# Gates made by VectorE's 32x32 block transposes, and the T1 sums moved from GpSimd to VectorE

## The reference, cut to what matters

```python
def _L1_ffn_ref(x, base_W, router_W, lora_A, lora_B):
    base = jnp.einsum('bsd,od->bso', x, base_W)
    logits = jnp.einsum('bsd,ed->bse', x, router_W)
    probs = jax.nn.softmax(logits.astype(jnp.float32), axis=-1)
    top_vals, top_idx = jax.lax.top_k(probs, 2)
    rw = top_vals / jnp.sum(top_vals, axis=-1, keepdims=True)
    w_dense = jnp.sum(jax.nn.one_hot(top_idx, 8) * rw[..., None], axis=-2)
    mid = jnp.einsum('bsd,edr->bser', x, lora_A)      # 8 experts x rank 16
    mid = mid * w_dense[..., None]
    return base + jnp.einsum('bser,erd->bsd', mid, lora_B) * 2
x = x + _L0_ffn_ref(_L0_cond_ref(x, ...), ...)
x = x + _L1_ffn_ref(_L1_cond_ref(x, ...), ...)
```

## Time and profile before

| | us |
|---|---|
| median of 3 runs | 687.29 |
| lowest and highest | 687.27, 687.53 |
| the profiled execution, first to last instruction | 685.8 |
| TensorE matmuls busy in it | 680.0 (3309 matmuls) |
| VectorE busy | 421.5 |
| ScalarE busy | 233.5 |
| GpSimd busy | 261.3 |
| granted TensorE clock | 1.000 throughout |

### The profile page before, as it was taken

The page is one execution under the profiler, slowest core; times in us unless marked ns, Lnnn a source line. Parts: engine busy times, 40 slices in busy tenths (PEclk is TensorE's granted clock), DMA queues, the critical chain, the costliest instruction groups (busy, mean ns, idle before and its releaser), DMA issues.

```text
span 685.8 us, 9221 instructions
## 1 busy us (share of the span) xinstructions
PE 680.0 (99%) x3309; PEld 600.7 (88%) x3309; DVE 421.5 (61%) x705; ACT 233.5 (34%) x429; POOL 261.3 (38%) x217
## 2 busy tenths in 40 slices
PE   8999999999999999999999999999999999999997
PEld 7999999888888888888899999998888888888886
DVE  5664668768855473862663753886698437738423
ACT  6444245644131034220514344266252302422200
POOL 2373023027593150395133432030647625105920
PEclk9999999999999999999999999999999999999999
DMA  8355756992868934547742755689836886535633
GB/s 298 109 159 180 261 198 209 390 380 108 263 186 321 343 117 130 157 141 258 281 170 72 231 169 183 246 275 375 332 122 216 291 333 195 175 117 171 192 113 122
DMA packets 74131, 147.24 MB, mean 215 GB/s; under 512 B 6948, under 2 KB 38308, under 8 KB 73958
## 3 DMA queue, kind: packets, MB, share of 16 engines
q1 hardware_dynamic: 70678, 138.20, 59.0%
q10 hardware_dynamic: 1872, 6.36, 3.0%
q0 software_dynamic: 1536, 2.10, 1.1%
HBM read 98.42 MB, written 47.33 MB: 213 GB/s over the span
## 4 chain that ended last, share of the span: by engine, by line
PE 97%; DMA 1%; SPq 1%; ACT 0%; DVE 0%; issue 0%
PE ps L599 45%; PE ps L481 15%; PE ps L482 15%; PE ps L483 15%; PE ps L558 4%; PE ps L615 2%; DMA e_raw<-in_ext 1%; PE ps L608 1%; SPq L281 0%; PE ps L498 0%; PE ps L581 0%; ACT e_hl L710 0%; SPq L258 0%; DVE w_hl L972 0%; DVE w L1177 0%; ACT w_hl L719 0%
## 5 line engine op out<-in xcount | busy, mean ns | idle before, releaser
L599 PE MATMUL ps<-x_hl,a_hl 128*128 128x512 f32 x1344 | 317.7, 394 | 0.0
L599 PEld LDWEIGHTS ps<-x_hl,a_hl 128*128 128x128 f32 x1344 | 251.1, 188 | 53.6 <-issue 0.3
L481 PE MATMUL ps<-e_hl,w_hl 128*128 128x384 f32 (+1 forms) x432 | 145.8, 338 | 0.6 <-DVE e_hl L972 0.5
L482 PE MATMUL ps<-e_hl,w_hl 128*128 128x384 f32 (+1 forms) x432 | 145.8, 338 | 0.0
L483 PE MATMUL ps<-e_hl,w_hl 128*128 128x384 f32 (+1 forms) x432 | 145.6, 337 | 0.0
L481 PEld LDWEIGHTS ps<-e_hl,w_hl 128*128 128x128 f32 x432 | 81.5, 189 | 1.8 <-issue 1.0
L482 PEld LDWEIGHTS ps<-e_hl,w_hl 128*128 128x128 f32 x432 | 81.4, 188 | 0.0
L483 PEld LDWEIGHTS ps<-e_hl,w_hl 128*128 128x128 f32 x432 | 81.4, 188 | 0.0
L972 DVE TENSOR_TENSOR x_hl<-x_raw,x_hl 128x512 fp32r<-128x512 f32 x64 | 60.8, 1004 | 8.9 <-ACT x_hl L806 8.9
L1353 POOL TENSOR_TENSOR w<-x_raw 128x512 f32<-128x512 f32 x16 | 23.8, 1515 | 104.6 <-DMA x_raw<-in_xT 34.0
L972 DVE TENSOR_TENSOR w_hl<-w_raw,w_hl 128x1024 fp32r<-128x1024 f32 (+2 forms) x24 | 20.6, 869 | 57.2 <-ACT w_hl L697 50.3
(11 more groups left out here) (115 smaller groups left out, 900.1 us busy)
## 6 DMA issues: line engine op xcount, KB each, us to landing
a_hl<-form_scratch SPq DMA_DIRECT2D x112, 512.0 KB, 5.2
form_scratch<-f_hl SPq DMA_DIRECT2D x56, 512.0 KB, 7.4
e_raw<-in_ext SPq DMA_DIRECT2D x12, 580.0 KB, 8.6
w_raw<-in_w ACTq DMA_DIRECT2D x12, 512.0 KB, 3.3
x_raw<-in_xT SPq DMA_DIRECT2D x6, 1024.0 KB, 8.0
x_raw<-x_scratch SPq DMA_DIRECT2D x6, 1024.0 KB, 7.0
x_scratch<-x_raw SPq DMA_DIRECT2D x16, 256.0 KB, 3.1
out_T<-x_raw SPq DMA_DIRECT2D x16, 256.0 KB, 3.3
```

The costliest lines, as they stand in the source:

```text
L481: nc.tensor.matmul(dst, w_hi, m_hi, start=start, stop=False, skip_group_check=again)
L482: nc.tensor.matmul(dst, w_hi, m_lo, start=False, stop=False, skip_group_check=again)
L599: last = nc.tensor.matmul(ps[:, bank, :], a_hl[:, n % NM, k, w, :], x_hl[:, slot, k, x, :], start=start and i == 0, stop=i == 3 * KH - 1, ...
```

## The change

The router's eight columns are copied 16 times side by side into a stationary tile `rt_cols` (ScalarE, one copy for each chunk). One 128x512 matmul ahead of the inner matmul then gives each token's logits 16 times over the partitions. VectorE's block transpose turns this into `by_token` [128, 16 groups, 32]: 32 tokens of a group on a quarter of the partitions, the eight logits beside each other. `routing` works on [128, 16, 8] instead of [128, 4, 8], finds the maxima by reduce and compare instead of max and index, writes the gates into `by_token` and transposes them by blocks again into `hg`. `gated` then reads the inner product from PSUM directly. Logit products, gate transposes, ScalarE's copy `inner` and GpSimd's `make_t1` are gone; VectorE makes T1.

```diff
             def inner_low(l, g, tb):
...
+                pe.wait_ge(S["rt_done"], u + 1)
+                nc.tensor.matmul(ps[:, S_BANK, :], rt_cols[:], low_mv[tb][:], start=True,
+                                 stop=True).then_inc(S["pe_logit"], 1)
                 nc.tensor.matmul(ps[:, H_BANK, :], stack[tb][:, D:D + ER], low_mv[tb][:], start=False,
                                  stop=True).then_inc(S["pe_h"], 1)
...
             def product(g, j, m, bank, start):
...
-                if gates_of is not None:
-
-                    pe.wait_ge(S["h_done"], 2 * g + gates_of + 1)
-                    pe.wait_ge(S["gate_done"], 2 * g + gates_of + 1)
...
-                    if logits_of is not None and i < TT:
-                        tb = logits_of
-                        logit = nc.tensor.matmul(ps[:, S_BANK, i * NE:(i + 1) * NE], low_mv[tb][:, i * P:(i + 1) * P],
-                                                 stack[tb][:, D + ER:EXT], start=True, stop=True)
...
-                    if gates_of is not None and i < TT:
-                        gate = nc.tensor.transpose(ps[:, H_BANK, i * P:(i + 1) * P], gates[:, i, :], ident_sb[:])
...
                         for m in (m2, m2 + 1):
                             pe.wait_ge(S["w5_done"], KH * g + m + 1)
                             product(g, W3, m, BANK_C12[m], False)
-                            if m == 0:
-                                pe.wait_ge(S["hg_lo"], 2 * g + 2)
-                            low_and_experts(0, 1, m, BANK_C12[m])
+                            if m >= 2:
+                                low_and_experts(0, 1, m, BANK_C12[m])
+                        if m2 == 0:
+                            pe.wait_ge(S["hg_lo"], 2 * g + 2)
+                            for m in range(2):
+                                low_and_experts(0, 1, m, BANK_C12[m])
...
+            def router_cols(l, g, tb):
...
+                if u:
+
+                    act.wait_ge(S["hg_done"], u)
+                nc.scalar.copy(rt_cols[:].rearrange("p (n e) -> p n e", e=NE),
+                               stack[tb][:, D + ER:EXT].bitcast(f32).unsqueeze(1).broadcast_to([P, P // NE, NE])
+                               ).then_inc(S["rt_done"], 1)
...
                     adapters(l, g, 1, more)
-                    t1_split(g, range(2))
-                    inner(g, 1)
-                    t1_split(g, range(2, 3))
+                    router_cols(l, g, 1)
+                    t1_split(g)
                     top_exp(g, 1)
-                    t1_split(g, range(3, 4))
                     keep_w5(g, 0)
...
+            def make_t1(g):
+
+                dve.wait_ge(S["pe_hx"], 2 * g + 2)
+                for k in range(KH):
+                    dve.wait_ge(S["t2_done"], KH * g + k + 1)
+                    sub(x_sum[:, SLOT_OF[g % SUPER][T1], k, 1, :], raw_of(B22, k), c21[:, k, :]
+                        ).then_inc(S["t1_done"], 1)
...
+                ins = nc.vector.transpose(by_token[:].rearrange("p g c -> p (g c)"), ps[:, S_BANK, :])
+                ins.then_inc(S["logit_read"], 1)
+                dve.wait_ge(S["logit_read"], u + 1)
+                chain(nc.vector.tensor_tensor(lg, lg,
+                                              bias_r[:].unsqueeze(1).broadcast_to([P, GR, NE]), ALU.add))
+                for i, (v, m, gate) in enumerate(((lg, ma, ga), (lg2, mb, gb))):
+                    chain(nc.vector.tensor_reduce(top[i][:], v, AXIS.X, ALU.max))
+                    chain(nc.vector.tensor_tensor(m[:], v, over(top[i], NE), ALU.is_equal))
+                    if i:
+                        sub(gap[:], top[1][:], top[0][:]).then_inc(S["gap_done"], 1)
+                    chain(nc.vector.tensor_tensor(m[:], m[:], ranks, ALU.mult))
+                    chain(nc.vector.tensor_reduce(first_of[i][:], m[:], AXIS.X, ALU.max))
+                    if i == 0:
+                        chain(nc.vector.tensor_tensor(m[:], over(first_of[i], NE), ranks, ALU.is_equal))
+                        chain(nc.vector.scalar_tensor_tensor(lg2, m[:], -3.0e38, lg, op0=ALU.mult, op1=ALU.add), False)
+                    chain(nc.vector.tensor_tensor(gate[:], over(first_of[i], WANT), wanted, ALU.is_equal))
                 dve.wait_ge(S["exp_done"], u + 1)
                 chain(nc.vector.tensor_scalar(den[:], ex[:], 1.0, None, ALU.add))
                 chain(nc.vector.reciprocal(wb[:], den[:]))
                 chain(nc.vector.tensor_scalar(wa[:], wb[:], 2.0, None, ALU.mult))
...
+                chain(nc.vector.tensor_tensor(den[:], ex[:], wa[:], ALU.mult), False)
+                chain(nc.vector.tensor_tensor(ga[:], ga[:], over(wa, WANT), ALU.mult))
+                chain(nc.vector.tensor_tensor(gb[:], gb[:], over(den, WANT), ALU.mult))
+                chain(nc.vector.tensor_tensor(by_token[:].rearrange("p g (n r) -> p g n r", r=R),
+                                              *(m[:].unsqueeze(3).broadcast_to([P, GR, WANT, R]) for m in (ga, gb)),
+                                              ALU.add))
+                chain(nc.vector.transpose(hg[:], by_token[:].rearrange("p g c -> p (g c)")))
...
+                dve.wait_ge(S["pe_h"], u + 1)
+                nc.vector.scalar_tensor_tensor(hg[:], ps[:, H_BANK, :], bias_sb[:, KT:KT + 1], hg[:],
                                                op0=ALU.add, op1=ALU.mult).then_inc(S["hg_done"], 1)
-                dve.wait_ge(S["hg_hi"], u + 1)
+
+            def gated_low(g, tb):
+                dve.wait_ge(S["hg_hi"], 2 * g + tb + 1)
                 sub(hg_hl[:, tb, 1, :], hg[:], hg_hl[:, tb, 0, :].bitcast(f32)).then_inc(S["hg_lo"], 1)
...
                     low_rest(g, 1)
+                    make_t1(g)
                     out_c11(g, 2)
                     out_c11(g, 3)
-                    made_split(g, T1, range(2))
-                    routing(g, 1)
-                    made_split(g, T1, range(2, 4))
-                    sum_split(g, T3, w57)
-                    for m in range(KH):
+                    made_split(g, T1)
+                    sum_split(g, T3, w57)
+                    routing(g, 1)
+                    gated(g, 1)
+                    keep_u2(g, 0)
+                    gated_low(g, 1)
+                    for m in range(1, KH):
                         keep_u2(g, m)
-                    gated(g, 1)
```

More of the change, by code:

```diff
@@ L39 @@
 SUPER = NCH // 2
+SQ = 32
+GR = CH // SQ
+WANT = SQ // R
 CHAIN = 13
@@ L185, in fused_layers @@
         assert 2 * E_PITCH <= 5 * CH
-        gates = place("gates", [P, TT, ER], f32, at[0] - CH * 4)
-        h_sb = place("h_sb", [P, CH], f32)
+        by_token = place("by_token", [P, GR, SQ], f32)
+        rt_cols = place("rt_cols", [P, P], f32r, at[0] - CH * 4)
         low_b = place("low_b", [LOW, CH], f32)
@@ L205, in fused_layers @@
         ids_sb = place("ids_sb", [1, LAYERS * BATCH], mybir.dt.int32)
[L206 to L216, removed]
+        lg, lg2 = (by_token[:, :, i * NE:(i + 1) * NE] for i in range(2))
+        top = [place(f"top{i}", [P, GR, 1], f32) for i in range(2)]
+        first_of = [place(f"first_of{i}", [P, GR, 1], f32) for i in range(2)]
+        gap = place("gap", [P, GR, 1], f32)
+        ex = place("ex", [P, GR, 1], f32)
+        den = place("den", [P, GR, 1], f32)
+        wa, wb = first_of
         assert at[0] <= nc.sbuf_usable_end, at[0] - nc.sbuf_usable_end
@@ L314, in load_const @@
                 sp.dma_start(ids_sb[:], ids).then_inc(S["d_ids"], 16)
[L315 removed]
+                for dst, src in ((ident_sb[:], ident), (iota_sb[:], iota[:, 0, :]), (smask_sb[:], smask),
                                  (halves_sb[STACK:P, :], smask[0:LOW, :]),
@@ L645, in _ @@
                         inner_low(l, g, 0)
-                        product(g, W1, 1, BANK_C11[1], True, logits_of=0)
-                    product(g, W1, 2, BANK_C11[2], True, logits_of=None if s else 0)
+                        product(g, W1, 1, BANK_C11[1], True)
+                    product(g, W1, 2, BANK_C11[2], True)
                     product(g, W1, 3, BANK_C11[3], True)
@@ L650, in _ @@
                         pe.wait_ge(S["w1_done"], KH * g + m + 1)
-                        product(g, W2, m, BANK_C11[m], False, gates_of=None if m else 0)
+                        product(g, W2, m, BANK_C11[m], False)
                     pe.wait_ge(S["hg_lo"], 2 * g + 1)
@@ L660, in _ @@
                             pe.wait_ge(S["out_done"], out_of(m - 1))
-                        product(g, W6, m, BANK_U2[m], True, logits_of=1 if m == 1 else None)
+                        product(g, W6, m, BANK_U2[m], True)
                         if m == 0:
@@ L669, in _ @@
                                 pe.wait_ge(S["u2_done"], KH * g + m - 1)
-                            product(g, W5, m, BANK_C12[m], True, gates_of=None if m else 1)
+                            product(g, W5, m, BANK_C12[m], True)
                         for m in (m2, m2 + 1):
@@ L845, in adapters @@
                     s_split(l, 2 * (g % SUPER) + tb + 1)
```

(28 more changed lines are left out.)

45 lines of the change are left out of this document (14 added, 31 removed).

## The result

| | before | after |
|---|---|---|
| median of 4 runs each, us | 687.28 | 693.05 |
| lowest to highest, us | 687.04 to 687.53 | 692.70 to 696.72 |
| profiled execution, span, us | 685.8 | 691.2 |
| TensorE busy, us (matmuls) | 680.0 (3309) | 676.6 (3253) |
| VectorE busy, us | 421.5 | 455.7 |

The ratio is 1.0094, 95% interval 1.0081 to 1.0107: slower, by 0.9%. The forecast was 691.1, in a range of 685.0 to 696.8.

The account below looks back on a forecast made before the run. TensorE was taken as the bound, busy 680.0 of 685.8 us. Savings of -5.7 us plus stalls 2 x 1.3 + 2.9 + 3.9 gave +3.8: 689.6 profiled, 691.1 us with 1.5 outside it, range 685.0 to 696.8.

Parts of the forecast that it names:

- TensorE's part: On TensorE: 64 small products gone, 7.5 us, and eight 128x512 matmuls added, 1.8; net -5.7 us.
- no stall: TensorE never waits ahead of W3 m=2, all 5.7 us are kept: 681.6 us; chance in full 0.08.
- The place: TensorE idle ahead of W3 m=2 once per superstep, released by ScalarE's `keep_w5`, queued behind the T4 splits.
- a wait ahead of W3 m=1: On TensorE: sign that the prediction is wrong, meaning a gate chain over 8 us.
- The gate chain: VectorE's linked steps in `routing`: 7.2 us, with each block transpose counted as one pass.
- rival (C): VectorE's block transposes cost the upper bound, 0.7 us more each, 5.6 in all: 696.7 us; chance 0.13.
- slack: Before the change, `keep_w5` could have ended at 304.5 and W3 m=2 began at 308.7: 4.2 us.
- The port: Shared SBUF port: `add_12` 0 starts 0.03 us ahead of `gated_low`, which waits for its end; a race.
- Rival (B): The shared port goes to `gated_low` first, each stall is 0.8 us smaller: 687.9 us; chance 0.17.
- The stalls: TensorE ahead of W3 m=2: 1.3 us in g=1 and g=3, 3.9 in g=0, 2.9 in g=2.
- `s_split`: In even supersteps it falls beside `add_12` and costs GpSimd 0.45 us more.
- The ring tile behind the load of B21: SyncE's queue: held free because the stall covers it; without cover a us or two in each even superstep.

Follow-up runs that it names:

- e7: Kernel of e1, with the load of the next B21 moved behind the three ring loads on SyncE's queue: 682.26 us, ratio 0.9926.
- e1: Changed kernel, with ScalarE's third and fourth `keep_w5` placed between the T4 splits instead of behind all four: 685.39 us, ratio 0.9970.
- e3: Changed kernel, with `gated_low` behind all four `keep_u2` instead of behind the first: 691.07 us, ratio 1.0053.
- e5: Changed kernel, with the last block transpose of `routing` written twice, linked, so the gate chain is 0.73 us longer: 696.96 us, ratio 1.0153.
- e4: Changed kernel, with T1's sums given back to GpSimd and the gates as changed: 700.64 us, ratio 1.0198.

## Why the prediction was right

- **TensorE's part, -5.7 us.** Right. With the stalls gone but for two waits of 0.4 (e7) the median is 5.2 us under that of before, in the same set of runs (687.47 - 682.26), and 0.7 over the 681.6 that I gave for no stall.
- **The place.** Right: W3 m=2, behind `keep_w5` 2, behind the T4 splits, once in each superstep. e1 shows the queue, e3 the link to GpSimd, e5 the link to the gates. One sign of being wrong did appear in small: a wait ahead of W3 m=1, 0.25 us in g=2. I had said that it would mean a gate chain over 8 us, and the chain took 7.45; I had looked for a wait like it in g=0.
- **The gate chain, 7.2 us.** It took 287.60 to 295.05, 7.45. The block transpose is one pass, 0.71 us for 512 columns, so rival (C) falls, and with it the 1.24 us that I had estimated from the bf16 figure of the Trainium skill, VectorE: DVE Perf Modes, "The three transpose paths". `routing` started at R+17.9 (I had 17.8). In the kernel before the chain took 287.54 - 283.52 = 4.0 us:

```profile
283.52 0.18 DVE L1139 TENSOR_TENSOR lg<-ps,bias_r 128x32 f32<-128x32 f32 x1
...
287.54 1.28 DVE L972 TENSOR_TENSOR x_hl<-x_sum,x_hl 128x512 fp32r<-128x512 f32 x2
...
291.15 2.48 DVE L975 TENSOR_TENSOR u<-ps,u 128x512 f32<-128x512 f32 x4
```

- **What made T4 late.** The last T4 sum ended at R+33.9 before (303.30 - 269.44) and at R+39.0 after, 5.1 us later, of which 4.2 were slack. By the rows, 3.4 of it are the longer gate chain, 0.7 is `gated`, which now stands ahead of `keep_u2` 0 (295.05 to 295.71) and stood behind `keep_u2` 3, and 0.8 is `gated_low` between the `keep_u2` (e3). The other 0.2 isn't assigned. So three tenths of the shift are VectorE's new order and not the chain's length. No run puts `gated` back behind `keep_u2`; what that would save is an estimate from these rows.
- **The port.** The race went the way that I had taken, `add_12` 0 first by 0.01 us (296.47 against 296.48), `gated_low` then took 1.83 and `add_12` 1 started at t+3.94 (3.9). Rival (B) did not occur: in all four supersteps of this profile, and of those of e1, e4, e5 and e7, `add_12` 0 comes first by 0.01 or 0.02 us, so nothing here shows a race that goes both ways. e3, where the two are kept apart, gains 2 us in the median, and not the 3.4 that its sum gave.
- **The stalls.** Forecast 3.9, 1.3, 2.9 and 1.3. Measured as the start of W3 m=2 less R less 38.53, which is what it takes without a stall (in e7, 300.50 + 5.44 - 267.41, the 5.44 being the 24 matmuls of W5 m=2 and 3): in g=1 309.85 - 269.67 - 38.53 = 1.65. In the same way, with R at 157.11, 495.83 and 610.72, 2.72 in g=0, 3.45 in g=2 and 1.65 in g=3: 9.5 in all. (The rows show 8.5 us idle, since they count from the modelled end of the last matmul, 0.16 later than its spacing.) I had 9.4 (9.5 before rounding, hence the 3.8 of my sum), and that the sums agree is luck: the four are off by -1.2, +0.35, +0.55 and +0.35. `routing` started at R+18.8 in g=0, where I had 20.0, and at R+19.6 in g=2, where I had 19.0; and `s_split` cost the three `add_12` beside it 0.2 and not 0.45 (3.97 against 3.79). I had put g=0 a microsecond behind g=2 from one profile of the token loads, and these move. GpSimd's waits for the loads of B22 in g=0 and g=2 were before, and then after:

```profile
POOL w L1353 <- DMA x_raw<-in_xT: 34.0, 1, 34.0
POOL w L1353 <- DMA x_raw<-x_scratch: 32.9, 1, 32.9
```

```profile
POOL w L1386 <- DMA x_raw<-x_scratch: 33.4, 1, 33.4
POOL w L1386 <- DMA x_raw<-in_xT: 32.1, 1, 32.1
```

- **What was missing.** -5.7 + 9.5 gives 3.8, and the span grew by 5.4. The difference is, within 0.1, the 1.7 us of the lower clock behind the longest stall. The prediction treated a stall as time lost once. The step that failed is its silence on the restart: it left TensorE's clock at full speed, as it was in all rows of before, where TensorE never stopped once it was under way.
- **The ring tile behind the load of B21**, held free because of the stall, was so; e1 took the stall away and had to pay for it, 0.5 and 0.8 us in its profile and 685.39 - 682.26 = 3.1 in the median of all runs, within the "us or two in each even superstep" of the prediction.

What stays open: which stalls the clock answers. In the four profiles with such stalls (after, e3, e4, e5) it never fell behind 1.49 us or less, fell once of twice behind 1.93 and once of twice behind 2.21 us, once of three times behind 2.50 and 2.55, and four times of five behind 2.71 to 2.77. Executions of one kernel differ too: of e5's four, one had a mean granted clock of 1.000 and took 695.91 us, and one had 0.990 and took 701.25. No run here separates more.

## What to carry to other kernels

When the busiest engine never waits, taking work from it is worth just the spacing of its instructions, but whoever takes the work over must be followed through every queue that it passes: here a gate chain 3.4 us longer reached the matmuls by way of an in-order list on ScalarE, in which a ready PSUM copy stood behind a late split. Before giving such a change up, look for the instruction that is ready and queued behind one that is not, and let it pass: two such reorderings, the first of which is worth nothing in the kernel before, made the same change 1.6% faster. And count a stall of TensorE of about 2 us or more at its length and, when the clock falls behind it, 1.7 us more; one in e4 cost 2.8 more.

## What the runs showed of the hardware that I had not expected

- The lower clock after stalls of 1.9 to 2.8 us. Its price in the first twelve matmuls was 1.6 us in the profiles of the kernel after and of e3 (4.61 against 3.01 to 3.03), and up to 2.5 us in e4 (5.49), where from one product's start to the next's it was 547.83 - 541.28 = 6.55 us against 317.23 - 313.47 = 3.76 at full clock. Kernels with such stalls are also uneven: the kernel after took 692.70 to 696.72 us and e4 698.80 to 703.50, where e7, which has none, took 681.86 to 682.76. The granted clock of the single runs goes with it: in the kernel after it was 0.998 in the three runs up to 693.25 us and 0.995 in the one of 696.72.
- A VectorE instruction that comes 0.01 us behind GpSimd's took 1.83 us, of which 0.6 is its own work, and GpSimd's own took 1.29, where one took 1.26 (5.03 / 4) with VectorE idle; the one that comes first pays next to nothing. The Trainium skill, SBUF — State Buffer, "SBUF: two separate sides", has it so.
- A linked step of 128 columns, a reduce or a two-input one, is 0.32 us from start to start (288.35 to 288.67), of which some 0.13 is the data: the 512-column pass of 0.69 has 384 columns more than the 0.29 of 128, which makes 1.04 ns for a column. The chain has twenty-three steps, eleven of them of 128 columns, nine shorter and three of 512, and most of it is fixed cost.
